# Last layer of a four-layer graph network: the node's own part recomputed on TensorE instead of prepared beside the neighbour sums

## The reference, cut to what matters

```
h_neigh = segment_sum(h[src], dst, N)
out = (h_neigh + h) / (deg + 1)[:, None]
out = out @ W.T + b
a = sigmoid(alpha)
out = out * a + h * (1 - a)
out = layernorm(out) * gamma + beta
x = layernorm(h + out)
```

## Time and profile before

| | us |
|---|---|
| median of 2 timed runs | 6418.26 (6416.53 to 6419.99) |
| the profiled execution's own time | 6385.53 |
| its span, first to last instruction | 6383.7 |

### The profile page before, as it was taken

One profiled execution on the slowest core, in us unless ns is written; L12 is line 12 of the kernel. 1 busy time (PEld: TensorE's weight loads), 2 busy tenths in 40 slices (PEclk: granted clock), 3 DMA queues, 4 the chain that ended last, 5 costly groups with the idle time before them and its releaser, 6 DMA issues. The chain is left out here.

```text
span 6383.7 us, 72084 instructions
## 1 busy us (share of the span) xinstructions
PE 3667.7 (57%) x20430; PEld 2870.6 (45%) x20430; DVE 3775.7 (59%) x11276; ACT 2488.0 (39%) x5939; POOL 2868.4 (45%) x2733
## 2 busy tenths in 40 slices
PE   5777741548832376621456523555699993775543
PEld 1344421447721255520455513444467772664443
DVE  9666630449944466522455574555567772665998
ACT  0233320438830155520122202444366662222776
POOL 0456667005557533376555504666155554453000
PEclk9888865769965589865677755666799996888666
DMA  8455531759957777621344445676344552786564
GB/s 322 133 151 154 155 124 38 269 182 302 311 155 257 249 256 256 215 80 46 113 121 119 116 177 149 222 233 231 127 164 171 178 173 78 251 273 216 208 208 164
DMA packets 704791, 1172.84 MB, mean 184 GB/s; under 512 B 110626, under 2 KB 453717, under 8 KB 698082
## 3 DMA queue, kind: packets, MB, share of 16 engines
q1 hardware_dynamic: 593024, 958.95, 45.9%
q0 software_dynamic: 103200, 183.16, 9.6%
q10 hardware_dynamic: 8172, 26.13, 1.1%
HBM read 689.93 MB, written 490.39 MB: 185 GB/s over the span
## 5 line engine op out<-in xcount | busy, mean ns | idle before, releaser
L2145 POOL DMA_INDIRECT sc_rows<-layer,node_idx x400 | 380.2, 950 | 298.8 <-DVE sc_xin L2160 145.2
L1978 PE MATMUL ro_end<-vals,end_mask 128*2 128x128 f32 x1600 | 248.2, 322 | 376.2 <-DVE vals L1842 238.7
L1337 POOL DMA_INDIRECT cap_own<-layer,w_own x200 | 205.7, 1028 | 489.5 <-SPq L1317 439.6
L2754 PE MATMUL tf_o_ps<-tf_w,tf_hidden 128*128 128x128 f32 (+1 forms) x3136 | 362.8, 276 | 10.6 <-issue 10.4
L2618 POOL DMA_INDIRECT tf_edge_x<-x,tf_src_idx x200 | 192.2, 961 | 387.7 <-SPq L2601 338.6
L2754 PEld LDWEIGHTS tf_o_ps<-tf_w,tf_hidden 128*128 128x128 f32 (+1 forms) x3136 | 356.9, 192 | 12.9 <-issue 12.9
L2742 PE MATMUL tf_h_ps<-tf_x_t,tf_w 128*128 128x512 f32 x784 | 350.7, 600 | 17.0 <-ACT tf_hidden L2703 15.8
L2703 ACT ACTIVATE tf_hidden<-tf_h_ps,tf_b 128x512 f32<-128x512 f32 x392 | 268.9, 687 | 231.2 <-PE tf_h_ps L2742 191.3
L1978 PEld LDWEIGHTS ro_end<-vals,end_mask 128*2 128x2 f32 x1600 | 150.2, 98 | 463.9 <-DVE vals L1842 247.6
L2004 PE MATMUL ro_acc<-vals,ro_mask 128*126 128x128 f32 x1600 | 243.3, 316 | 195.4 <-ACT ro_square L1936 99.7
L710 POOL DMA_INDIRECT msg_rows<-values,s_eid x200 | 209.8, 1049 | 295.0 <-POOLq L70 234.4
(11 more groups left out here) (484 smaller groups left out, 11809.9 us busy)
## 6 DMA issues: line engine op xcount, KB each, us to landing
ro_mask<-masks SPq DMA_DIRECT2D x100, 504.0 KB
layer<-zeros SPq DMA_DIRECT2D x96, 512.0 KB
si_both<-layer SPq DMA_DIRECT2D x48, 1024.0 KB
ro_far<-far SPq DMA_DIRECT2D x75, 512.0 KB
ro_both<-both SPq DMA_DIRECT2D x75, 512.0 KB
agg<-zeros SPq DMA_DIRECT2D x48, 512.0 KB
x<-zeros SPq DMA_DIRECT2D x48, 512.0 KB
mom_x<-in_x_dram SPq DMA_DIRECT2D x48, 512.0 KB
```

Source lines behind the costliest of these rows:

```text
L1978: mm = nc.tensor.matmul(end_ps[0:2, j, :], k.end_mask[:, t, :], k.vals[:, t, :], start=True, stop=True, skip_group_check=True)
L2145: nc.gpsimd.indirect_dma_start(out=rows[:, g % SC, c * GT + j, :], out_offset=None, in_=k.layer1, in_offset=bass.IndirectOffsetOnAxis(ap=k ...
L2754: mm = nc.tensor.matmul(o_ps[h][0:p, j, :], hidden[:, h, b, j * P:j * P + p], w2[:, b, :], start=b == 0, stop=b == NB - 1)
```

## The change

`OwnPart` is gone, and with it all its stages beside the neighbour sums and the tables `own` and `shifted`. `LastWeights` takes its place; it is set up between the two stages and prepares a W turned, `stay` = (1-a) times the identity, gamma, and the bias and beta as rows split in three bf16 parts (`split_biases`, 9 chained VectorE instructions for each bias).

In `mean_layer_phase` a block now loads agg and x3. TensorE's list in step m is `turn(m)`, `product(m-1)`, `lay(m-2)`:
- `turn`: for each of 8 node columns two accumulating float32 matmuls, agg and x3 as the stationary operand, against `share`, the identity times 1/degree, which VectorE makes for each block (`divide`). The result is (agg + x3)/degree, turned. ScalarE copies it.
- `product`: into PSUM `z`, for each half a bf16 matmul that lays the bias, then for each column x3 times `stay` and the turned sum times a W. This is the layer's result itself; VectorE (`measure`) and ScalarE read it in PSUM.
- `lay`: into PSUM `base`, of which there is one, for each half a bf16 matmul that lays beta, and for each column x3 times the identity. `add` reads it in place of `shifted`. `lay(n)` waits until `add(n-1)` has ended.

VectorE's list in step m is: `divide(m+1)`, the scales for m-2 and m-4, gamma for m-3, `measure(m-1)`, `add(m-3)`.

```diff
-class OwnPart:
+class LastWeights:
...
+        self.w_t, self.gamma, self.stay = sb("w_t", [P, D]), sb("gamma", [P, D]), sb("stay", [P, P])
+        rows, mix = sb("rows", [3, 2, D]), sb("mix", [P, 4])
         with ExitStack() as inner:
-            w_ps = k.ps(inner, "op_w_ps", [P, 512])
-            s = {x: k.sem(inner, "op_" + x) for x in ("w_turned", "w_step", "w_exp")}
+            w = k.sb(inner, "lw_w", [P, D])
+            load_constants(k, [(w[:, :], a["L3_gnn_W"]), (rows[:, 0, :], a["L3_gnn_b"].partition_broadcast(3)),
+                               (rows[:, 1, :], a["L3_gnn_beta"].partition_broadcast(3)),
+                               (self.gamma[:, :], a["L3_gnn_gamma"].partition_broadcast(P)),
+                               (mix[:, 0:1], a["L3_gnn_alpha"].partition_broadcast(P))])
+            w_ps = k.ps(inner, "lw_w_ps", [P, 512])
...
+                    c.link(v.tensor_scalar(self.stay[:, :], k.ident[:, :], mix[:, 3:4], None, ALU.mult))
...
+        self.bias, self.beta = split_biases(k, st, "lw_bias", [rows[:, 0, :], rows[:, 1, :]])
...
+XL = 4
-        agg, own, shifted = (sb(x, [P, ML, NJ, D]) for x in ("agg", "own", "shifted"))
-        z, scaled, total, res = (sb(x, [P, 2, NJ, D]) for x in ("z", "scaled", "total", "res"))
-        norms = [Norm(k, st, "ml_norm0", floor=own_part.floor), Norm(k, st, "ml_norm1")]
-        conv = Linear(k, st, "ml_conv", own_part.w_t[:, :])
-        names = (["z_made", "normed", "gained", "added", "res_made", "stored0", "stored1"]
-                 + [f"{x}_in{u}" for x in ("agg", "own", "shifted") for u in range(ML)])
-        s = {x: k.sem(st, "ml_" + x) for x in names}
-
-        def nth(n):
-            return n // ML * 16 + 16
+        agg, x = sb("agg", [P, ML, NJ, D]), sb("x", [P, XL, NJ, D])
+        share, turned = (sb(name, [P, 2, NJ, P]) for name in ("share", "turned"))
+        scaled, total, res = (sb(name, [P, 2, NJ, D]) for name in ("scaled", "total", "res"))
+        norms = [Norm(k, st, f"ml_norm{m}") for m in range(2)]
+        turned_ps = k.ps(st, "ml_turned_ps", [P, NJ, P])
+        z = [k.ps(st, f"ml_z{u}", [P, NJ, D]) for u in range(2)]
+        base = k.ps(st, "ml_base", [P, NJ, D])
+        names = (["shared", "turned", "copied", "z_made", "based", "normed", "gained", "added", "res_made", "stored0",
+                  "stored1"] + [f"agg_in{u}" for u in range(ML)] + [f"x_in{u}" for u in range(XL)])
...
-                def load(tile, table, what, free):
-                    def stage(n):
-                        u, p = n % ML, tail(n)
-                        if n >= ML:
-                            sp.wait_ge(free, n - ML + 1)
-                        sp.dma_start(tile[0:p, u, :, :], node_rows(table, n, p)).then_inc(s[f"{what}_in{u}"], 16)
-                    return stage
+                def load(n):
+                    u, q, p = n % ML, n % XL, tail(n)
+                    if n >= ML:
+                        sp.wait_ge(s["turned"], n - ML + 1)
+                    sp.dma_start(agg[0:p, u, :, :], node_rows(k.agg, n, p)).then_inc(s[f"agg_in{u}"], 16)
+                    if n >= XL:
+                        sp.wait_ge(s["based"], n - XL + 1)
+                    sp.dma_start(x[0:p, q, :, :], node_rows(k.x3, n, p)).then_inc(s[f"x_in{q}"], 16)
...
+                pipeline(NG + 1, (load, 0), (store, 5))
...
-                dve.sem_inc(conv.free, 1)
-
-                def gather_up(n):
-                    u, q, p = n % 2, n % ML, tail(n)
-                    dve.wait_ge(s[f"own_in{q}"], nth(n))
-                    dve.wait_ge(conv.made, n + 2)
+
+                def divide(n):
                     if n >= 2:
-                        dve.wait_ge(s["normed"], n - 1)
-                    for b in range(2):
-                        ins = v.tensor_tensor(z[0:p, u, 4 * b:4 * b + 4, :], own[0:p, q, 4 * b:4 * b + 4, :],
-                                              conv.out[b][0:p, :, :], ALU.add)
-                    ins.then_inc(s["z_made"], 1)
+                        dve.wait_ge(s["turned"], n - 1)
+                    v.tensor_tensor(share[:, n % 2, :, :], k.ident[:, :].unsqueeze(1).broadcast_to([P, NJ, P]),
+                                    k.dinv2[:, n * NJ:n * NJ + NJ].unsqueeze(2).broadcast_to([P, NJ, P]),
+                                    ALU.mult).then_inc(s["shared"], 1)
+
+                def measure(n):
+                    u, p = n % 2, tail(n)
                     dve.wait_ge(s["z_made"], n + 1)
-                    dve.sem_inc(conv.free, 1)
-                    norms[0].statistics(dve, n, u, p, z[:, u, :, :])
+                    norms[0].statistics(dve, n, u, p, z[u])
...
-                    v.tensor_tensor(total[0:p, u, :, :], scaled[0:p, u, :, :], shifted[0:p, q, :, :],
-                                    ALU.add).then_inc(s["added"], 1)
+                    for b in range(2):
+                        ins = v.tensor_tensor(total[0:p, u, 4 * b:4 * b + 4, :], scaled[0:p, u, 4 * b:4 * b + 4, :],
+                                              base[0:p, 4 * b:4 * b + 4, :], ALU.add)
+                    ins.then_inc(s["added"], 1)
...
-                pipeline(NG + 1, (negate(0), 2), (negate(1), 4), (gain, 3), (gather_up, 1), (add, 3))
+                divide(0)
+                pipeline(NG + 1, (lambda n: n < NG and divide(n + 1), 0), (negate(0), 2), (negate(1), 4), (gain, 3),
+                         (measure, 1), (add, 3))
...
+                def copy(n):
+                    u, p = n % 2, tail(n)
+                    act.wait_ge(s["turned"], n + 1)
+                    if n >= 2:
+                        act.wait_ge(s["z_made"], n - 1)
+                    for b in range(2):
+                        ins = nc.scalar.activation(turned[:, u, 4 * b:4 * b + 4, 0:p], turned_ps[:, 4 * b:4 * b + 4, 0:p],
+                                                   ACT.Copy)
+                    ins.then_inc(s["copied"], 1)
...
                 def turn(n):
-                    pe.wait_ge(s[f"agg_in{n % ML}"], nth(n))
-                    conv.turn(pe, n, tail(n), agg[:, n % ML, :, :])
-
-                pipeline(NG + 1, (turn, 0), (lambda n: conv.product(pe, n, tail(n)), 0))
-        clear_semaphores(nc, [x for norm in norms for x in norm.sems] + conv.sems + list(s.values()))
+                    u, p = n % 2, tail(n)
+                    pe.wait_ge(s[f"agg_in{n % ML}"], n // ML * 16 + 16)
+                    pe.wait_ge(s[f"x_in{n % XL}"], n // XL * 16 + 16)
+                    pe.wait_ge(s["shared"], n + 1)
+                    if n:
+                        pe.wait_ge(s["copied"], n)
+                    for j in range(NJ):
+                        nc.tensor.matmul(turned_ps[:, j, 0:p], agg[0:p, n % ML, j, :], share[0:p, u, j, 0:p], start=True,
+                                         stop=False)
+                        mm = nc.tensor.matmul(turned_ps[:, j, 0:p], x[0:p, n % XL, j, :], share[0:p, u, j, 0:p],
+                                              start=False, stop=True)
+                    mm.then_inc(s["turned"], 1)
+
+                def rows_of(parts, p, b, into):
+                    nc.tensor.matmul(into[0:p, 4 * b:4 * b + 4, :].rearrange("p j d -> p (j d)"), k.ones_bias[:, 0:p],
+                                     parts[:, :, :].rearrange("p j d -> p (j d)"), start=True, stop=False,
+                                     skip_group_check=True)
+
+                def product(n):
+                    u, p = n % 2, tail(n)
+                    pe.wait_ge(s["copied"], n + 1)
+                    if n >= 2:
+                        pe.wait_ge(s["normed"], n - 1)
+                    for b in range(2):
+                        rows_of(last.bias, p, b, z[u])
+                        for j in range(4 * b, 4 * b + 4):
+                            nc.tensor.matmul(z[u][0:p, j, :], last.stay[0:p, 0:p], x[0:p, n % XL, j, :], start=False,
+                                             stop=False, skip_group_check=True)
+                            mm = nc.tensor.matmul(z[u][0:p, j, :], turned[:, u, j, 0:p], last.w_t[:, :], start=False,
+                                                  stop=j == 4 * b + 3, skip_group_check=True)
+                    mm.then_inc(s["z_made"], 1)
+
+                def lay(n):
+                    p = tail(n)
+                    if n:
+                        pe.wait_ge(s["added"], n)
+                    for b in range(2):
+                        rows_of(last.beta, p, b, base)
+                        for j in range(4 * b, 4 * b + 4):
+                            mm = nc.tensor.matmul(base[0:p, j, :], k.ident[0:p, 0:p], x[0:p, n % XL, j, :], start=False,
+                                                  stop=j == 4 * b + 3, skip_group_check=True)
+                    mm.then_inc(s["based"], 1)
+
+                pipeline(NG + 1, (turn, 0), (product, 1), (lay, 2))
...
-        own_part = OwnPart(k, st)
-        with ExitStack() as meaning:
-            own_part.begin(meaning)
```

(61 more changed lines are left out.)

72 lines of the change are left out of this document (9 added, 63 removed).

## The result

| | us |
|---|---|
| kernel before, median of 2 runs | 6418.26 |
| changed kernel, median of 2 runs | 6605.77 (6601.01 to 6610.54) |
| ratio | 1.0271 [1.0241, 1.0302] |
| profiled execution of the changed kernel: its time, its span | 6610.54, 6608.8 |

Slower by 187.5 us, where 156 was forecast. The two profiled executions differ by 225 us, and 66 of these came before the change begins: the last scatter of the phase before starts at 5445.90 us now and at 5379.67 then, in code that the change doesn't touch. The other 159 us lie between that scatter and the last store.

What follows compares the result with a forecast made beforehand. Bounds taken: the own part's traffic and queues in the neighbour sums, VectorE in the last layer. 328 us lost in the last layer, 172 gained in the sums, 0 fixed: 156 on 6418 gives 6574 us, range 6440 to 6640.

Steps and rivals of the forecast that it cites:

- stage 1, scatters first to last: Neighbour sums without the own part: GpSimd paces 200 scatters, 264 us, 172 us less.
- fixed parts: Setup and clearing around the two phases: 7 us added against 7 us saved, nothing, within 8 us either way.
- stage 2: Last layer: 47 steps of 17.0 us plus start and end, 836 us in place of 508, 328 more.
- The new wait: Last layer: TensorE's lay(m-2) waits for add(m-3), queued behind measure(m-1); 4.54 us with drain, added to 9.74 of work.
- Rival 2: Last layer: add(m-3) is reached before the product ends, waits overlap, step 10.2 us; 6276 us, faster; chance 0.06.
- The clock: Last layer: TensorE's clock falls in each gap, rises 5.4 us after work begins, 2.7 us more a step.
- the new gap is as long, so each step will begin cold: Last layer: TensorE's gap matches the old 4.6 us, so every step starts at the low clock, making 17.0 us.
- rival 3: Neighbour sums: landing, row loads or the copy chain pace a group at 6.8 us; gain 97 us, 6650; chance 0.08.
- I take 1.32 us: Neighbour sums: time assumed for each scatter, near the undisturbed 1.27, giving 200 x 1.32 = 264 us.

Runs made afterwards that it cites:

- add_first: The changed kernel with VectorE's last two list entries exchanged, add(m-3) ahead of measure(m-1): 6248.60 us, ratio 0.9817 to the kernel before.
- fill_wait: The changed kernel with 14 spare TensorE matmuls between the product and the wait for the add: 6445.01 us, ratio 1.0111 to the kernel before.
- after_again: The changed kernel, unaltered, run again on another chip: 5927.86 us, ratio 1.024 to the kernel before on that chip.
- s1_warm: add_first with two spare matmuls ahead of each carried sum of the neighbour sums: 6265.96 us, ratio 0.9825 to the kernel before.
- four_sums: add_first with four buffers in place of three for rows and sums of the neighbour sums: 6240.19 us, ratio 0.9799 to the kernel before.
- one_scatter: add_first with one scatter in place of four for each group of neighbour sums, output incomplete: 6116.34 us in one run.
- tail_early: add_first with the last block of nodes loaded early into buffers of its own: 6245.37 us, ratio 0.9788 to the kernel before.
- scatter_none: add_first with the indices of the neighbour sums' scatters beyond the table, so no row is written; run twice on the other chip: 5640.68 and 5622.14 us.
- no_beside: The kernel before with only the own part left out beside the neighbour sums, last layer loading x3 instead: 6225.91 us, ratio 0.9769 to the kernel before.

## Why the prediction was right

It said 6574 us, slower by 2.4%; measured were 6605.77 and 2.7%. By its own terms, against the profiled execution:

| term | predicted | measured | where |
|---|---|---|---|
| stage 1, scatters first to last | 264 (-172) | 297.7 (-139) | 5466.24 to 5763.95 |
| fixed parts | 0 | 0 | 10.4 less ahead, 10.8 more behind |
| stage 2 | 836 (+328) | 805.3 (+297) | 5790.28 to 6595.6 |
| sum | +156 | +159 | |
| phases not touched | 0 | +66 | 5379.67 to 5445.90 |

**The new wait** was read from the two lists alone, and it is there 44 times in the 720 us: 4.16 us each, where 4.29 was worked out (4.54 less the 0.25 of the drain). That add_first removes all of it shows that order is its cause, and not the add's own length, which add_first keeps. Rival 2, which stood for overlap, was priced at 10.2 us a step and 142 us faster. With its condition met it is 9.79 us and 123 faster, bound by TensorE (9.74 us were worked out) and not by VectorE's list. In stage 2 that run loses 14 us where the rival booked 30, and these 14 are the last block's slow loads; in stage 1 it gains 141 where the rival had 172. The unknown cost of the statistics from PSUM was booked at nothing: eight take 1.68 us, and took 1.65 from SBUF.

**The clock** is where stage 2 was mis-sized. The step "the new gap is as long, so each step will begin cold" holds, but I took one pair of edges for all steps, 5.4 us and so 2.7 us lost. By fill_wait it is 2.1 on the mean; by the low stretches of the trace it is 1.35 in the shortest step and 3.0 in the longest: (17.0 - 16.25) x 45 is the 34 us by which the steps fell short. Start and end took 3 us more. The Trainium skill (TensorE: Matmul & The Clock Gate, What's actually happening), which was weighed there, puts the penalty of the ramp under 1% of a typical kernel. The trace does not agree: in this kernel it is 100 of 6606 us, 1.5%, in stage 2 alone, because the gap comes back in every step.

**Stage 1** was mis-sized the other way, by 34 us, nearly half of the way to rival 3 (a gain of 97 us in place of 172). The step is "I take 1.32 us". In the result's profile 138 of the 199 distances between scatters are at most 1.35 us, together 178 us, 49 are from 1.35 to 2, together 74, and 12 are over 2, together 45 us. The first two kinds are the undisturbed scatter and the one beside VectorE's masks, 1.35 us on the mean of both. The last kind is GpSimd standing for a late tile, some 30 us more than 12 scatters would take. The prediction has handovers that pace the stage in rival 3 alone, and nothing of them in its own sum. In after_again there is none of it, and the stage took 268 us. So the price of the scatters held, and the term lacked the late tiles. Their cause is open. The low clock and the number of buffers are excluded (s1_warm, four_sums). They are gone with three quarters of the scatters (one_scatter), yet the kernel before has one of them beside all 200. And they show in the result's profile and in every one of add_first to tail_early but one_scatter, in none of the four profiles of the last chip. Whether the writes to HBM or GpSimd's own accesses do it was to be told by scatter_none, and wasn't.

The two errors cancel: stage 1 gained 34 us less than forecast, and stage 2 lost 31 us less. That the sum comes within 3 us is luck; each mechanism held, and each size was off. On the chip without late tiles the change costs 137 us (5927.86 - 5790.59). That is near what a stage 1 without them would give (159 - 30 = 129), but the kernel before has no profile there, so this isn't shown. Of the result's 187.5 us, some 28 are in neither stage of these two traces (187.5 - 159); with two timed runs of each, and 66 us between two profiled executions in untouched code, I leave them unexplained.

## What to carry to other kernels

When a change adds a wait between two engines, write both lists down and look for a stage that each has ahead of what the other waits for: here `add(m-3)` behind `measure(m-1)` and `lay(m-2)` behind `product(m-1)` made two engines of 55% and 74% take turns, and swapping two entries turned 2.7% slower into 1.8% faster. An older unit's work goes ahead of a younger unit's wherever the younger has to be waited for. Moving work onto an idle engine only pays if its list can run ahead; and a gap that returns in each step is to be priced with the clock after it, here half as much again as the wait itself.

## What was not expected of the hardware

- The kernel before took 6418, 6372 and 6373 us in three launches and 5790.59 us in the fourth, on another chip. In the changed kernel's traces four of the phases account for 624 of the 667 us that it saves there ahead of stage 1, and stage 2 saves nothing; ratios moved far less (1.0271 and 1.024).
- In the result's profile and in the first two groups of runs TensorE's signal to ScalarE in a serial chain came about 1 us later for one tile in five to eight (37 of 196 in the result's profile, 24 of 196 in no_beside), in runs of several in a row and at either clock. It did so with all 200 scatters in the stage, not with 50 of them, and but once in the kernel before, which has the 200 too.
- An indirect scatter that writes no row takes GpSimd as long as one that writes 128 (1.33 and 1.34 us from one to the next).
- A load of 106 partitions had two of the 16 DMA engines busy, ran at 44 to 66 GB/s and took 20 us, where whole blocks load at 418 GB/s; issued two steps of 16 us ahead in the changed kernel, it is hidden, and it is in the open once a step takes 10.
- With a strictly periodic gap of 4.2 us the clock fell once in every step and came back 2.7 to 6.0 us after work had begun, in a pattern that repeats over four or five steps (15.4, 15.8, 16.8, 16.9 us, at times a 17.0).
